# Preln attention and expert block on one core: gates multiplied into the expert activations on GpSimd, experts summed in PSUM, maxima split before they are transposed, query copy on ScalarE, statistics first

## The chip, the cores and the metric

The kernel runs on one core of a Trainium2 chip. The metric is the device time in microseconds (us) of one execution. Before the change the median of 3 executions is 1236.5 us (1234.62 to 1236.58).

## What is computed

32 batches of 256 tokens with 128 channels pass through one transformer layer: attention with 16 heads and a rational function in place of the exponential, then 4 experts of which each token takes 2.

```python
# x: 32 x 256 x 128, float32
def stablemax3(logits):                       # per head, over the keys
    x = logits - max(logits)
    s = 1 / (1 - x * (1 - 0.5 * x * (1 - x / 3)))   # x <= 0 here
    return s / sum(s)

x = x + attention(layernorm(x))               # q k^T * 8**-0.5, stablemax3, times v, w_out, b_out
xf = layernorm(x)
probs = softmax(xf @ router_w + router_b)     # 4 experts
gates = the two largest of probs, divided by their sum, zeros elsewhere
h = silu(xf @ w1[e]) * (xf @ w3[e])           # e = 0..3, 512 hidden channels each
x = x + sum_e gates[:, e] * (h[e] @ w2[e])
```

## The kernel before

Every engine has its own instruction stream, written out by hand; semaphores join them, and nothing reorders an engine's stream. The work is a pipeline over batches. Step `n` of the outer loop (`over_batches`) runs `first_half` and then `second_half` on each engine, and works on several batches at once: the queries, keys and statistics of batch n+2 or n+1, the attention of batch n, the projection, router and first expert unit of batch n-1, and the experts of batch n-2. One step is called a trip here; there are 36 of them (n = -2 to 33), and all stages are full from n = 2 to 30.

**First half of a trip.** TensorE makes, in turn, the "distances" of batch n (scores minus the row maximum, 8 units of 128x1024 into the two halves of the PSUM tile `sc`) and the expert units 1 to 7 of batch n-2 (`up_a`, `up_b`: each unit is 256 hidden channels of w1 and of w3, as three float32r products). ScalarE squares a unit of distances (`w_sq`, L464) and takes the silu of `up_a` (L472). VectorE makes the polynomial (`poly`, L603) and multiplies silu by `up_b` into `hid` (`hidden`, L595). GpSimd splits the queries and keys into a high and a low part (`qk_split`, L367 and L370); SyncE writes them to DRAM (`qk_scratch`) and reads them back in 12 transfers in the layout of `q_stack` and `k_pad`.

**Second half.** TensorE makes 8 units of scores of batch n+1 (`scores`, L963), and VectorE takes each unit's maxima (`scores_max`, L716); a later unit of scores waits for the maxima of the unit two before it. Between the scores stand the down projections of the experts of batch n-2 (`down(e)`, L982, into `up_a` or `up_b` in turn); VectorE scales each by its gate and adds it (`add_expert`, L733). VectorE aggregates the statistics (L704, L707), GpSimd and ScalarE make 1/sqrt(variance) of them and GpSimd normalizes (`xn2`, `xn`, L414). TensorE transposes `xn2` (`router_operand`, L1025). After the eighth maxima TensorE transposes `mx` (`maxima_T`, L999), VectorE splits the transposed maxima into a high and a low part (`split_maxima`, L756 and L758), and SyncE copies the two into the last rows of `q_stack`; the distances of the next first half need them. The first expert unit of batch n-1 (`up_a_unit`, `up_b_unit`) stands between `maxima_T`, `router_logits` (L1035) and `queries_operand` (L1010). ScalarE takes the logarithm of `poly` (`log_of`, L521) and its exponential (`weights_of`, L526), two units at a time, with the two small instructions of the statistics (L537, L540) between the second logarithm and the first exponential. The order of VectorE in this half is

```python
for u in range(U):
    if has(i, off + 1):
        scores_max(u)
    if u == 0:
        statistics()
    if u in (1, 3) and has(i, off - 2):
        add_expert(u // 2)
    if u == 4 and has(i, off - 1):
        router_T()
# then add_expert(2), split_maxima(), add_expert(3), route_logits(), queries_T(), the comparisons
```

## Time and profile before

| | |
|---|---|
| median of 3 executions | 1236.5 us |
| profiled execution: its own time, its span | 1235.11 us, 1233.4 us |
| TensorE busy | 1137.5 us, 92% |
| VectorE busy | 1029.9 us, 84% |
| ScalarE busy | 1015.2 us, 82% |
| GpSimd busy | 333.2 us, 27% |
| mean granted TensorE clock | 0.983 |

The profiled execution took 1235.11 us, of which 1233.4 us lie between its first and last instruction. The profile names TensorE as PE, VectorE as DVE, ScalarE as ACT, GpSimd as POOL and SyncE as SP; PEld is the weight load of TensorE, which overlaps its matmuls. The ends of matmuls are modelled in the trace: two that follow each other without a stall overlap in their rows, so a stall is best read from the distance of two starts. A float32 matmul stands as two records, with one weight load each.

### The profile page before, as it was taken

To read this page: it belongs to the slowest core of one execution; us is meant where nothing else is said; L and a number is where in the kernel's file an instruction comes from. 1 tells how busy PE (TensorE), PEld (TensorE's weight loads), DVE (VectorE), ACT (ScalarE), POOL (GpSimd) and SP (SyncE) were. 2 spreads that over 40 slices of the span, in tenths; PEclk is the share of its full clock that TensorE was granted. 3 is DMA by queue.
4 is the path that set the end of the run, shared out by engine and by line. 5 is a ranking of instruction groups with operands and counts; after the bars stand their busy time and mean duration, and the time that the engine had idled before them with its cause. 6 is when DMAs were issued, how large, how long until landed. Compare 5 with 4: busy or idle time off the path is not lost.

```text
span 1233.4 us, 29285 instructions
## 1 busy us (share of the span) xinstructions
PE 1137.5 (92%) x10116; PEld 980.6 (80%) x10116; DVE 1029.9 (84%) x1998; ACT 1015.2 (82%) x1070; POOL 333.2 (27%) x707
## 2 busy tenths in 40 slices
PE   2577999999999999999999999999999999999988
PEld 1345888888888888888888888888888888888877
DVE  3777889888888988888898888889888888988833
ACT  1478888888898888888888888898888889888872
POOL 5113322222332222233222132322312233231111
PEclk9877999999999999999999999999999999999999
DMA  5111111222111122211112221111122111121000
GB/s 173 57 56 49 44 57 57 67 65 65 46 46 48 55 65 65 65 48 43 48 55 65 65 65 51 41 48 55 65 65 65 53 40 46 56 64 62 11 6 9
DMA packets 83689, 67.97 MB, mean 55 GB/s; under 512 B 6664, under 2 KB 82120, under 8 KB 83656
## 3 DMA queue, kind: packets, MB, share of 16 engines
q1 hardware_dynamic: 83080, 67.01, 17.1%
q10 hardware_dynamic: 576, 0.52, 0.2%
q8 instruction: 20, 0.33, 0.1%
q14 instruction: 13, 0.11, 0.0%
HBM read 45.42 MB, written 20.97 MB: 54 GB/s over the span
## 4 chain that ended last, share of the span: by engine, by line
PE 59%; issue 11%; DVE 10%; POOL 7%; ACT 6%; DVEq 3%; DMA 2%; SPq 1%; POOLq 1%; ACTq 0%
PE up_a L807 13%; PE up_b L807 9%; PE sc L873 9%; PE pv L823 5%; DVE mx L716 5%; PE up_b L982 4%; PE pv L807 4%; POOL xn L414 4%; PE up_a L982 3%; DVEq L705 3%; PE sc L963 2%; DVE poly L603 2%; PE misc L1016 2%; ACT silu_a L472 2%; ACT poly L521 2%
## 5 line engine op out<-in xcount | busy, mean ns | idle before, releaser
L464 ACT ACTIVATE w_sq<-sc 128x1024 f32<-128x1024 f32 x256 | 259.2, 1026 | 142.8 <-PE sc L873 133.7
L716 DVE TENSOR_REDUCE mx<-sc 128x4 f32<-128x1024 f32 x256 | 304.6, 1214 | 41.4 <-PE sc L963 41.4
L603 DVE SCALAR_TENSOR_TENSOR poly<-w_sq,sc 128x1024 f32<-128x1024 f32 x256 | 310.7, 1215 | 33.3 <-ACT w_sq L464 26.8
L521 ACT ACTIVATE poly<-poly,two 128x2048 f32<-128x2048 f32 x128 | 251.9, 1992 | 0.4
L526 ACT ACTIVATE poly<-poly 128x2048 f32<-128x2048 f32 x128 | 239.6, 1895 | 0.0
L873 PE MATMUL sc<-q_stack,k_pad 128*128 128x256 f32 x1024 | 170.1, 294 | 7.1 <-DVE poly L603 7.0
L472 ACT ACTIVATE silu_a<-up_a 128x512 f32<-128x512 f32 x256 | 153.0, 598 | 21.2 <-PE up_a L807 14.3
L807 PE MATMUL up_a<-xn_hi,w_hi 128*128 128x256 f32 x512 | 156.1, 305 | 7.0 <-ACT silu_a L472 2.8
L873 PEld LDWEIGHTS sc<-q_stack,k_pad 128*128 128x128 f32 x1024 | 141.4, 192 | 11.8 <-DVE poly L603 9.4
L807 PE MATMUL up_a<-xn_hi,w_lo 128*128 128x256 f32 x512 | 144.4, 282 | 0.0
L807 PE MATMUL up_a<-xn_lo,w_hi 128*128 128x256 f32 x512 | 143.8, 281 | 0.0
L982 PE MATMUL up_a<-w_sb,hid 128*128 128x128 f32 x1024 | 138.7, 284 | 5.4 <-ACT silu_a L472 5.1
L381 POOL TENSOR_TENSOR x_resb<-x_res,b_out_all 128x128 f32<-128x128 f32 x64 | 27.8, 456 | 426.9 <-DVE y_acc L656 357.4
L982 PEld LDWEIGHTS up_a<-w_sb,hid 128*128 128x128 f32 x1024 | 121.3, 191 | 21.8 <-ACT silu_a L472 11.7
L963 PE MATMUL sc<-k_pad,q_stack 60*128 60x256 f32 x1024 | 105.1, 323 | 32.1 <-DMA k_pad<-qk_scratch 22.7
L823 PE MATMUL pv<-poly,v_pad 128*32 128x256 f32 x2048 | 133.1, 390 | 0.0
L982 PE MATMUL up_b<-w_sb,hid 128*128 128x128 f32 x1024 | 126.0, 277 | 0.0
L982 PEld LDWEIGHTS up_b<-w_sb,hid 128*128 128x128 f32 x1024 | 120.7, 194 | 0.0
L595 DVE TENSOR_TENSOR hid<-silu_a,up_b 128x512 f32<-128x512 f32 x160 | 108.7, 679 | 13.3 <-PE up_b L807 6.9
L963 PEld LDWEIGHTS sc<-k_pad,q_stack 60*128 60x128 f32 x1024 | 75.3, 197 | 52.2 <-DVE mx L716 14.7
L807 PEld LDWEIGHTS up_a<-xn_hi,w_hi 128*128 128x128 f32 x512 | 96.8, 189 | 18.3 <-DVE y_acc L733 10.8
L807 PEld LDWEIGHTS up_a<-xn_lo,w_hi 128*128 128x128 f32 x512 | 96.8, 189 | 0.0
(105 smaller groups left out, 2028.1 us busy)
## 6 DMA issues: line engine op xcount, KB each, us to landing
qk_scratch<-qk_split SPq DMA_DIRECT2D x32, 512.0 KB, 2.8
k_pad<-qk_scratch SPq DMA_DIRECT2D x256, 64.0 KB
q_stack<-qk_scratch SPq DMA_DIRECT2D x124, 128.0 KB
x_in<-in_L_attn_x_dram SPq DMA_DIRECT2D x32, 128.0 KB, 2.1
x_res<-in_L_attn_x_dram SPq DMA_DIRECT2D x32, 128.0 KB, 2.2
out_dram<-y_acc SPq DMA_DIRECT2D x32, 128.0 KB, 1.8
poly<-in_L_ffn_w_dram SPq DMA_DIRECT2D x2, 1024.0 KB, 6.7
q_stack<-m_split SPq DMA_DIRECT2D x64, 16.0 KB
```

The source lines that it names most:

```text
L464: nc.scalar.activation(w_sq[:, u % 2, :], sc[:, u % 2, :], ACT.Square).then_inc(sq_ok, 1)
L472: nc.scalar.activation(silu_a[:, u % 2, :], up_a[:], ACT.Silu).then_inc(silu_ok, 1)
L521: nc.scalar.activation(poly[:, C * g:C * (g + 1), :], poly[:, C * g:C * (g + 1), :], ACT.Ln, bias=two[:]).then_inc(ln_ok, 1)
L526: nc.scalar.activation(poly[:, C * g:C * (g + 1), :], poly[:, C * g:C * (g + 1), :], ACT.Exp, scale=-1.0).then_inc(p_ok, 1)
L595: nc.vector.tensor_tensor(hid[:, 2 * u:2 * u + 2, :].rearrange("p a t -> p (a t)"), silu_a[:, u % 2, :], b_bank[u], ALU.mult).then_inc(hid ...
L603: nc.vector.scalar_tensor_tensor(poly[:, u, :], w_sq[:, u % 2, :], 3.0, sc[:, u % 2, :], ALU.add, ALU.mult).then_inc(poly_ok, 1)
L716: nc.vector.tensor_reduce(by_row[:, :, 2 * g:2 * g + 2], sc[:, u % 2, :].rearrange("p (j k t) -> p j k t", j=2, k=2), AX.X, ALU.min, negat ...
L807: last = nc.tensor.matmul(dst, lhs[a], rhs[b], start=(k == 0), stop=(k == len(terms) - 1))
L823: last = nc.tensor.matmul(pv[32 * j:32 * j + 32, g // 2, :], v_pad[par][:, c, 4 * g + j, first:first + 32], poly[:, C * g + c, at:at + S], ...
L873: last = nc.tensor.matmul(sc[:, u % 2, at:at + S], k_pad[par][:, 2 * g + k, j, c * 128:(c + 1) * 128], q_stack[par][:, 2 * g + k, :], star ...
L963: last = nc.tensor.matmul(sc[:, u % 2, at:at + S], q_stack[par][rows, 2 * g + k, c * 128:(c + 1) * 128], k_pad[par][rows, 2 * g + k, j, :] ...
L982: last = nc.tensor.matmul(bank[:, c * D:(c + 1) * D], hid[:, FB * e + f, c * 128:(c + 1) * 128], w2_sb[:, FB * e + f, :], start=(f == 0), ...
```

## The change

The edits, on all five engines:

- **Gates.** The gate of a token and expert is no longer applied to the result of the down projection. VectorE makes the gates at the end of the second half of trip n (batch n-1). SyncE writes them to DRAM (`gate_scratch`) and, in the next first half, reads them back to all partitions (`gate_all`, 128 x 1024 values, 512 KB). GpSimd multiplies each of the 8 units of `hid`, 128x512, in place by the gates of its tokens; the second operand lies at a step of 8 values in `gate_all`.
- **Experts.** All four down projections add up in PSUM, chunk 0 in `up_b`, chunk 1 in `up_a`, and VectorE adds the sum once (`experts_added`) where `add_expert` had 8 instructions. `down(e)` waits for the gated units in place of `acc_ok`.
- **Maxima.** VectorE splits `mx` into `mx_split` (two instructions of 128x32) before the transposes; these then give both parts at once, one copy (`maxima_out`) takes them out of PSUM, and one transfer brings them to `q_stack` where there were two.
- **Router.** `router_logits` stands on TensorE right behind `down(3)`, ahead of `score(6)`; `route_logits` and `experts_added` stand on VectorE between the seventh and the eighth `scores_max`. `maxima_T` waits for `lg_ok` too, and `queries_operand` for `m_ok`.
- **Other moves.** The copy of queries and keys out of PSUM goes from VectorE to ScalarE, behind silu(0). `statistics()` stands ahead of the first `scores_max`. ScalarE's `exp_l` stands ahead of the last `weights_of`. GpSimd's `x_resb` goes from the first half to the end of the second.

```diff
 # SyncE, first half (at its start) and second half (at its end)
+                if has(i, off - 2):
+                    sp.wait_ge(gates_out, gates_at)
+                    after(sp, gated, gated_before)
+                    sp.dma_start(gate_all[:].rearrange("p t c e -> p (t c e)"),
+                                 row_to_all(gate_scratch, 128 * C * E)).then_inc(gates_in, 16)
...
-                    sp.wait_ge(m_hi_ok, m_split_at)
-                    sp.dma_start(q_stack[par][MROW::2, :, :].bitcast(F32),
-                                 m_split[:, 0, :].bitcast(F32)).then_inc(m_stacked[par], 16)
                     sp.wait_ge(m_ok, m_split_at)
-                    sp.dma_start(q_stack[par][MROW + 1::2, :, :].bitcast(F32),
-                                 m_split[:, 1, :].bitcast(F32)).then_inc(m_stacked[par], 16)
+                    sp.dma_start(q_stack[par][MROW:, :, :].bitcast(F32), m_split[:]).then_inc(m_stacked[par], 16)
...
+                if has(i, off - 1):
+                    par = (off - 1) % 2
+                    sp.wait_ge(gates_ok, gates_at)
+                    after(sp, gates_in, gates_read)
+                    sp.dma_start(gate_scratch, gates[par][:].rearrange("p c e -> p (c e)")).then_inc(gates_out, 16)
 # GpSimd, first half, behind the two qk_split instructions
+                if has(i, off - 2):
+                    m = no(i, off) - 2
+                    pool.wait_ge(gates_in, 16 * (m + 1))
+                    for u in range(UP):
+                        pool.wait_ge(hid_ok, UP * m + u + 1)
+                        h = hid[:, 2 * u:2 * u + 2, :].rearrange("p k (c t) -> p k c t", c=C)
+                        by_token = gate_all[:, :, :, 2 * u // FB].rearrange("p t c -> p c t")
+                        nc.gpsimd.tensor_tensor(h, h, by_token.unsqueeze(1).to_broadcast([128, 2, C, 128]),
+                                                ALU.mult).then_inc(gated, 1)
 # ScalarE, first half, behind silu(0)
+                    act.wait_ge(qk_full, m + 1)
+                    after(act, qk_ok, m)
+                    nc.scalar.copy(qk[:], misc[:]).then_inc(qk_out, 1)
 # VectorE, second half
+                def experts_added():
+                    m, par = n - 2, off % 2
+                    dve.wait_ge(down_full, m + 1)
+                    nc.vector.tensor_tensor(y_acc[par][:], up[:, :, 0:D], y_acc[par][:], ALU.add).then_inc(acc_ok, 1)
...
+                statistics()
                 for u in range(U):
                     if has(i, off + 1):
                         scores_max(u)
-                    if u == 0:
-                        statistics()
-                    if u in (1, 3) and has(i, off - 2):
-                        add_expert(u // 2)
                     if u == 4 and has(i, off - 1):
                         router_T()
-                if has(i, off - 2):
-                    add_expert(2)
+                    if u == 6 and has(i, off - 1):
+                        route_logits()
+                    if u == 6 and has(i, off - 2):
+                        experts_added()
                 if has(i, off + 1):
                     split_maxima()
-                if has(i, off - 2):
-                    add_expert(3)
-                if has(i, off - 1):
-                    route_logits()
+                if has(i, off - 1):
+                    compare()
+                if has(i, off + 1):
+                    maxima_out()
                 if has(i, off + 2):
                     queries_T()
                 if has(i, off - 1):
+                    for k in range(GATE):
+                        gate_step(k)
 # TensorE, second half
                 down(3)
+                if has(i, off - 1):
+                    router_logits()
                 score(6)
                 score(7)
...
                 if has(i, off - 1):
                     up_a_unit(i, off - 1, 0)
-                    router_logits()
                     up_b_unit(i, off - 1, 0)
```

**VectorE around the last maxima.** The instruction list of VectorE in a trip's second half, from the seventh maxima on (`mx`), in the kernel before:

```order
L716 TENSOR_REDUCE mx<-sc 128x2x2 [waits s_full] x3
L733 SCALAR_TENSOR_TENSOR y_acc<-up_a,gates,y_acc 128x128 [waits acc_ok,gates_ok,down_full]
L733 SCALAR_TENSOR_TENSOR y_acc<-up_a,gates,y_acc 128x128 [waits acc_ok]
L756 TENSOR_SCALAR m_split<-misc 16x256 [waits m_stacked1,mT_full]
L758 SCALAR_TENSOR_TENSOR m_split<-misc,m_split 16x256 [waits m_hi_ok]
L733 SCALAR_TENSOR_TENSOR y_acc<-up_b,gates,y_acc 128x128 [waits acc_ok,gates_ok,down_full]
L733 SCALAR_TENSOR_TENSOR y_acc<-up_b,gates,y_acc 128x128 [waits acc_ok]
L742 TENSOR_TENSOR logits<-misc,router_b_all 128x4 [waits gates_ok,lg_full]
L742 TENSOR_TENSOR logits<-misc,router_b_all 128x4
L746 TENSOR_REDUCE top_l<-logits 128x2 [waits lg_ok]
L749 TENSOR_TENSOR shifted<-logits,top_l 128x8 [waits exp_ok,top_ok]
```

And the same place in the changed kernel, whose first row holds the sixth and the seventh maxima:

```order
L714 TENSOR_REDUCE mx<-sc 128x2x2 [waits s_full] x2
L734 TENSOR_TENSOR logits<-misc,router_b_all 128x4 [waits gates_ok,lg_full]
L734 TENSOR_TENSOR logits<-misc,router_b_all 128x4
L738 TENSOR_REDUCE top_l<-logits 128x2 [waits lg_ok]
L741 TENSOR_TENSOR shifted<-logits,top_l 128x8 [waits exp_ok,top_ok]
L727 TENSOR_TENSOR y_acc<-up,y_acc 128x256 [waits down_full]
L714 TENSOR_REDUCE mx<-sc 128x2x2 [waits s_full]
L749 TENSOR_SCALAR mx_split<-mx 128x4x8 [waits mT_full,s_used]
L751 SCALAR_TENSOR_TENSOR mx_split<-mx,mx_split 128x4x8 [waits mx_hi_ok]
```

Five instructions (four of the router, one of the experts) now stand ahead of the eighth maxima, and two more behind it and ahead of what TensorE's transposes wait for.

**TensorE behind the last down projection.** The list of TensorE in the kernel before, from the end of `down(3)` (`w_sb`, `hid`) over the transposes of the maxima (`mx`) to the router's matmuls (`rw`):

```order
L982 MATMUL up_b<-w_sb,hid 128x128 x7
L963 MATMUL sc<-k_pad,q_stack 128x256 [waits s_used]
...
L999 MATMUL misc<-ident,mx 16x128 [waits xn2_out,s_used]
L999 MATMUL misc<-ident,mx 16x128
...
L807 MATMUL up_a<-xn_hi,w_hi 128x256 [waits xn2_lo_ok,acc_ok]
...
L1035 MATMUL misc<-rw,xn_T 128x4 [waits m_ok,xn2_out]
L1035 MATMUL misc<-rw,xn_T 128x4
```

And the same stretch in the changed kernel:

```order
L1000 MATMUL up<-w2_sb,hid 128x128 x7
L1053 MATMUL misc<-rw,xn2_T 128x4 [waits xn2_out]
L1053 MATMUL misc<-rw,xn2_T 128x4
...
L844 MATMUL pv<-poly,v_pad0 32x256 [waits p_ok]
L844 MATMUL pv<-poly,v_pad0 32x256 x7
L1018 MATMUL misc<-ident,mx_split 32x128 [waits lg_ok,mx_ok]
L1018 MATMUL misc<-ident,mx_split 32x128
L828 MATMUL up<-xn2_hi,w1_hi 128x256 [waits xn2_lo_ok,acc_ok,silu_ok]
```

The two router matmuls moved from behind the transposed maxima to ahead of the last two units of scores.

## Rows read from the trace of the kernel before

**Rows 1.** The page: span, and busy time of each engine.

```profile
span 1233.4 us, 29285 instructions
PE 1137.5 (92%) x10116; PEld 980.6 (80%) x10116; DVE 1029.9 (84%) x1998; ACT 1015.2 (82%) x1070; POOL 333.2 (27%) x707
```

**Rows 2.** Busy time in stretches: length, PE, PEld, DVE, ACT, POOL, clock.

```profile
130.50:1206.00 1075.50, 1040.39 (x9454) 905.99 (x9455) 934.35 (x1841) 933.01 (x981) 292.00 (x631) 1.00 0.17 53
```
```profile
884.00:902.00 18.00, 17.17 (x168) 13.75 (x167) 14.95 (x35) 17.55 (x14) 6.67 (x17) 1.00 0.06 16
902.00:920.00 18.00, 17.83 (x154) 16.58 (x153) 17.06 (x28) 13.95 (x20) 3.23 (x5) 1.00 0.29 95
```

**Rows 3.** Waits of the whole run: us in total, times, longest.

```profile
PEld misc L999 <- DVE mx L716: 26.0, 30, 1.8
PEld up_a L807 <- DVE y_acc L733: 10.8, 26, 0.4
```

**Rows 4.** Timeline of PE and PEld in a second half: start, length, instruction.

```profile
891.64 0.43 PE L1025 MATMUL misc<-ident,xn 128*128 128x128 f32 x2 [0.35 <-POOL xn L414]
891.91 1.95 PE L982 MATMUL up_b<-w_sb,hid 128*128 128x128 f32 x16
893.79 0.75 PE L963 MATMUL sc<-k_pad,q_stack 60*128 60x256 f32 x8
...
896.74 0.39 PE L999 MATMUL misc<-ident,mx 128*16 128x128 f32 x2 [0.35 <-DVE mx L716]
897.26 0.39 PE L807 MATMUL up_a<-xn_hi,w_hi 128*128 128x256 f32 x1
...
899.48 0.38 PE L1010 MATMUL misc<-ident,xn 128*128 128x128 f32 x2
```
```profile
898.14 0.52 PEld L1035 LDWEIGHTS misc<-rw,xn_T 128*128 128x128 f32 x4
```

**Rows 5.** Timeline of DVE, the same trip and its next first half.

```profile
892.30 0.41 DVE L692 COPY xn_T<-misc 128x256 f32<-128x256 f32 x1
...
894.33 2.36 DVE L716 TENSOR_REDUCE mx<-sc 128x4 f32<-128x1024 f32 x2 [0.49 <-PE sc L963]
...
897.17 0.41 DVE L756 TENSOR_SCALAR m_split<-misc 16x256 fp32r<-16x256 f32 x1
...
898.79 0.23 DVE L742 TENSOR_TENSOR logits<-misc,router_b_all 128x4 f32<-128x4 f32 x2 [0.25 <-PE misc L1035]
...
899.25 0.17 DVE L749 TENSOR_TENSOR shifted<-logits,top_l 128x8 f32<-128x8 f32 x1
...
919.54 0.68 DVE L595 TENSOR_TENSOR hid<-silu_a,pv 128x512 f32<-128x512 f32 x1
```

**Rows 6.** Timeline of ACT.

```profile
884.40 3.90 ACT L521 ACTIVATE poly<-poly,two 128x2048 f32<-128x2048 f32 x2
888.21 0.19 ACT L537 ACTIVATE ln_var<-var_eps 128x4 f32<-128x4 f32 x1
...
902.42 1.94 ACT L464 ACTIVATE w_sq<-sc 128x1024 f32<-128x1024 f32 x2 [0.70 <-PE sc L873]
904.25 0.60 ACT L486 COPY o_T<-pv 128x512 f32<-128x512 f32 x1
```

**Rows 7.** Timeline of POOL.

```profile
888.71 0.20 POOL L398 TENSOR_TENSOR newton<-rstd 128x4 f32<-128x4 f32 x1 [1.29 <-ACT rstd L540]
...
891.49 1.57 POOL L414 TENSOR_SCALAR xn<-x_in,mean_var,rstd 128x128 f32<-128x128 f32 x2
...
902.90 1.04 POOL L367 TENSOR_TENSOR qk_split<-qk,zero 128x512 fp32r<-128x512 f32 x1 [0.87 <-DVE qk L615]
904.02 1.30 POOL L370 TENSOR_TENSOR qk_split<-qk,qk_split 128x512 fp32r<-128x512 f32 x1
```

**Rows 8.** DMA issues: the page (KB, us to landing), SyncE's timeline.

```profile
qk_scratch<-qk_split SPq DMA_DIRECT2D x32, 512.0 KB, 2.8
```
```profile
910.79 4.93 SPq L311 DMA_DIRECT2D k_pad<-qk_scratch  x8
```

## Prediction before the run

> **What bounds the kernel now.** I read the page first for the span and the shares: TensorE is busy 92% of 1233.4 us, VectorE 84%, ScalarE 82%, GpSimd 27% [rows 1]. Shares over a run hide stages, so the busy times in stretches come next. From 130.5 to 1206.0 us the trips repeat: TensorE's wait before the transposed maxima occurs 30 times in the run [rows 3], once in each trip that has both a batch n+1 and a batch n-1 (n = 1 to 30), and 1075.5 / 30 = 35.85 us a trip, at full granted clock [rows 2]. Within one trip the two halves differ. From 902 to 920 TensorE is busy 17.83 of 18.00 us: the first half is TensorE's alone. From 884 to 902 it is busy 17.17 of 18.00 [rows 2]. So whatever a trip can lose or gain is in the second half, except for a few tenths.
>
> The timeline of TensorE shows where the second half waits. Its transposes of xn2 start at 891.64, after an idle 0.35 that GpSimd's normalization ended. The transposes of the maxima start at 896.74, after 0.35 idle for VectorE's maxima, and up_a follows only 0.52 later, where two such transposes need 0.27 (891.64 to 891.91) [rows 4]: the rest, 0.25, is the wait for add_expert(2), seen 26 times [rows 3].
>
> Who sets the 891.64? Not the statistics. ScalarE is in its two logarithms from 884.40 to 888.2 and takes ln_var right behind, at 888.21 [rows 6]; GpSimd had by then waited 1.29 us for ScalarE's result [rows 7]. From there to 891.64 it is a fixed chain of small instructions. And who sets the 896.74? From 891.64 the chain is down(3) (1.88 us, 891.91 to 893.79), scores unit 6 at 893.79, the last two maxima from 894.33, for which VectorE had sat idle 0.49 [rows 5], then the transposes. So in this half the order is: ScalarE, GpSimd, TensorE (down(3), scores), VectorE (two maxima), TensorE.
>
> **The change part by part.** I take the trip above and ask how far each of its marks moves, in us.
>
> Ahead of 891.64, nothing gained. Statistics first makes mean_var ready about 1.7 earlier, but ln_var still stands behind ScalarE's second logarithm. Down(0) no longer waits for silu(7), which lets TensorE start some 0.3 sooner; it then arrives earlier at the xn2 transposes and waits there longer. The two add_expert calls that leave VectorE's maxima 1 to 4 only lengthen its idle time before unit 6.
>
> From 891.64 to the transposed maxima, four things are put into the chain:
> - router_logits on TensorE, ahead of scores unit 6: 0.52, its four weight loads [rows 4].
> - route_logits on VectorE between maxima 6 and 7: from 898.79 to the end of the last of the four, 899.25 + 0.17 = 899.42, so 0.63 [rows 5]. Its input is ready, so no wait is added.
> - experts_added, one 128x256 sum from PSUM: 0.41, the row of the 128x256 copy out of PSUM [rows 5].
> - the split of mx, two dependent instructions of 128x32. Not in the trace. Below: two like the 128x8 row at 0.17, 0.34; above: two like the 16x256 split at 0.41, 0.82, plus a semaphore. The size is nearer the small one; I take 0.45.
>
> Together 2.0: the transposed maxima start 2.0 later, and nothing shortens that stretch, since what left VectorE had not been on it. In that time TensorE has no other work: it idles in front of them about 2.3 minus the 0.5 of the router, some 1.8.
>
> Behind it two things leave the chain before queries_operand (899.48 in the trace): the router's 0.52 between up_a and up_b, and the 0.25 of add_expert(2), since experts_added ran earlier. That is 0.77. The new wait of queries_operand for maxima_out costs nothing: the copy (0.41) lies beside up_a and up_b, 1.5 us; without that cover it would be its 0.41. So queries_operand, and with it the next first half, starts 2.0 - 0.77 = 1.2 later.
>
> The transfer of the maxima: one issue instead of two, behind a path of transposes, copy and issue that is no longer than before counted from the transposes. Since the transposes stand 0.77 nearer to the first half, the margin shrinks by this and grows by the saved issue; I count 0, with up to 0.5 on the upper side.
>
> First half. The query copy costs ScalarE 0.60, as o_T's copy of the same size, and lies in the 0.70 that ScalarE idles before its first square [rows 6], from about 902.0 on; the squares move by 0.2. VectorE loses the copy and four gate steps there, and reaches hidden(1) a tenth sooner. Since TensorE is full, I count -0.1. GpSimd gets eight products of 128x512. The gates come at about 901.5 (the query transposes at 899.48 [rows 4], a copy, four small steps); a write and a read through DRAM follow, each bounded by the 512 KB transfer at 2.8 us to landing [rows 8], so gate_all is there at about 907.5. One product: below 1.04 (second operand one repeated value), above 3.1 (the 128x128 normalization is 0.79, times four), and nearest 1.30, the row with two full operands [rows 7]; I take 1.30. Eight take 10.4, to 917.9, but the last unit of hid ends only at 920.2 [rows 5], so GpSimd ends at 921.5. Its next duty is var_eps, which ScalarE wants at 888.21 + 35.85 = 924.1. Margin 2.5 us: hidden. The limit is a product of (923.8 - 907.5) / 8 = 2.0 us.
>
> The queue of SyncE: it waits for gates_out until about 904.3, then issues gate_all, and the qk_scratch write is due at 905.3, when the split ends [rows 7]; behind it 12 stack transfers are issued until 915.7 [rows 8]. If gate_all delays these by a microsecond, they still land before the next scores at about 919.5, and behind these TensorE waits for xn2 anyway. Counted as 0; uncovered it would be at most the 2.8 of one such transfer in every trip. The edge trips are not changed by more than a few us: their down projections take 1.8 each, more than a product, so the gating keeps up.
>
> Sum: 1.2 - 0.1 = +1.1 a trip, 30 trips, +33 us. Against the profiled execution's 1235.1 that is 1268; the median of the runs shown stands 1.4 above that execution, so 1269.
>
> The Trainium skill, GPSIMD Engine Reference, section Performance pitfalls for Q7 kernels, says that a read with a step of more than 8 bytes costs about 2.9 cycles an element in place of 1.9, half as much again. No row here has a strided operand of this size. An estimate by that page: the product would take 1.3 times 1.5, about 2.0 us, right at the limit worked out above, and the sum would stay at 1269 or gain a few tenths a trip.
>
> **The rivals.**
> (B) GpSimd becomes the bound: a product takes well over 2.0 us, because of the stepped operand. For it: the 3.1 above, and the limit's closeness. Against: 1.30 in the nearest row. At 2.3 us GpSimd ends at 907.5 + 18.4 = 925.9, 2.1 past the limit, so +2.1 + 1.1 a trip: 1331. At 3.1: 932.3, +8.5 + 1.1: 1523.
> (C) Faster. The marks ahead of the transposed maxima move by less than the 0.77 that leaves the chain behind them. That is the point from which it decides. It would take router and expert instructions that cost VectorE a third of their rows' time, or an xn2 that comes earlier. The last can give at most what TensorE's idle time there gives, 0.35 + 0.3. Against it: ln_var's place behind the logarithms. If all of TensorE's waits in this half (0.3 at down(0), 0.35, 0.35, 0.25) went, it would be -1.2 a trip, 1199; half of that, 1217.
> (D) The change comes to nothing: growth ahead and gain behind balance, 1235 to 1239. For it only that small instructions in a row overlap somewhat.
>
> **How the numbers follow.** My forecast (A) has bounds of its own: lower, the split at 0.34, router and experts at two thirds of their rows, and 0.4 of waiting for xn2 gained: +0.35 a trip, 1247; upper, the split at 0.9, experts 0.6, and 0.5 for the maxima's transfer: +2.2, 1302. Chances: A 0.66, B 0.11, C 0.17, D 0.06. A measurement of this kernel can tell about 0.2% (2.5 us) from no change. Faster 0.17, same 0.06, slower 0.77. The range has to leave out no more than 0.2: from 1225, into the weaker cases of C, to 1302, which leaves out B and the strong cases of C.
>
> **What would show it.** In the profile after: the wait of the transposes on VectorE's mx_split at about 1.5 to 2 us in 30 trips; up_a right behind them without a wait for y_acc; VectorE idle about 1 us ahead of the seventh maxima; xn2's transposes still released by GpSimd, ln_var still right behind the logarithms; the product near 1.3 us and all eight done before var_eps is wanted; the first half no longer than 17.9 us. Wrong would be: a product above 2.0, ln_var waiting for GpSimd, scores waiting for k_pad, or transposed maxima less than 0.8 later against xn2's transposes than the 5.1 us now.

## Result and the profile after

The changed kernel takes 1246.7 us in the median (4 executions, 1245.46 to 1247.79) against 1236.5: the ratio is 1.0086, with a 95% interval of 1.0069 to 1.0103. It is slower, as forecast, but by 10 us and not by 33. The time lies inside the range of 1225 to 1302. The size is what missed: the measured loss is less than a third of the forecast one, and a trip lost 0.48 us where 1.1 was forecast.

The page of the changed kernel; the span and the shares, the chain that ended last, and the costliest group:

```profile
span 1245.4 us, 29490 instructions
...
PE 1112.9 (89%) x10116; PEld 975.4 (78%) x10116; DVE 960.7 (77%) x1774; ACT 1031.1 (83%) x1102; POOL 740.0 (59%) x963
...
POOL 32%; issue 20%; PE 20%; DMA 12%; DVE 9%; SPq 2%; ACT 2%; POOLq 1%; DVEq 0%
...
L396 POOL TENSOR_TENSOR hid<-hid,gate_all 128x512 f32<-128x512 f32 x256 | 410.2, 1618 | 130.2 <-DVE hid L624 75.1
```

Against [rows 1], VectorE lost 69 us of work and GpSimd gained 407. TensorE has the same 10116 matmuls and is busy less of a longer span. The chain now runs for a third through GpSimd. That looks like a verdict on the products, and it is not one, as an experiment shows below: the chain follows whatever was released last at each step, and says nothing of how close the second arrival was.

One trip, on each engine. TensorE, start and length in us; of the expert units only the first matmul of chunk 0 (904.38) and of chunk 1 (905.18) is shown:

```profile
897.46 0.44 PE L1045 MATMUL misc<-ident,xn 128*128 128x128 f32 x2 [0.82 <-POOL xn L429]
897.74 1.95 PE L1000 MATMUL up<-w_sb,hid 128*128 128x128 f32 x16
899.52 0.51 PE L1053 MATMUL misc<-rw,xn_T 128*128 128x4 f32 x4
899.96 0.74 PE L984 MATMUL sc<-k_pad,q_stack 60*128 60x256 f32 x8
900.63 1.93 PE L844 MATMUL pv<-poly,v_pad 128*32 128x256 f32 x32
904.23 0.40 PE L1018 MATMUL misc<-ident,mx_split 128*32 128x128 f32 x2 [1.67 <-DVE mx_split L751]
904.38 0.36 PE L828 MATMUL up<-xn_hi,w_hi 128*128 128x256 f32 x1
...
905.18 0.28 PE L828 MATMUL up<-xn_hi,w_hi 128*128 128x256 f32 x1
...
905.90 0.38 PE L1030 MATMUL misc<-ident,xn 128*128 128x128 f32 x2
...
908.00 1.29 PE L894 MATMUL sc<-q_stack,k_pad 128*128 128x256 f32 x8
...
933.71 0.43 PE L1045 MATMUL misc<-ident,xn 128*128 128x128 f32 x2 [0.84 <-POOL xn L429]
```

VectorE in the same second half:

```profile
900.51 1.22 DVE L714 TENSOR_REDUCE mx<-sc 128x4 f32<-128x1024 f32 x1 [1.01 <-PE sc L984]
901.65 0.22 DVE L734 TENSOR_TENSOR logits<-misc,router_b_all 128x4 f32<-128x4 f32 x2
...
902.18 0.42 DVE L727 TENSOR_TENSOR y_acc<-up,y_acc 128x256 f32<-128x256 f32 x1
902.52 1.21 DVE L714 TENSOR_REDUCE mx<-sc 128x4 f32<-128x1024 f32 x1
903.76 0.18 DVE L749 TENSOR_SCALAR mx_split<-mx 128x32 fp32r<-128x32 f32 x1
```

ScalarE and GpSimd at the end of the next first half:

```profile
926.48 3.90 ACT L550 ACTIVATE poly<-poly,two 128x2048 f32<-128x2048 f32 x2
930.28 0.19 ACT L566 ACTIVATE ln_var<-var_eps 128x4 f32<-128x4 f32 x1
```
```profile
926.61 1.54 POOL L396 TENSOR_TENSOR hid<-hid,gate_all 128x512 f32<-128x512 f32 x1 [0.68 <-DVE hid L624]
928.10 0.21 POOL L407 TENSOR_TENSOR var_eps<-mean_var,eps_all 128x4 f32<-128x4 f32 x1
```

Compared stretch by stretch with [rows 4] and [rows 5], and with the start of the first distances before, at 901.57 in this row:

```profile
901.57 0.70 PE L873 MATMUL sc<-q_stack,k_pad 128*128 128x256 f32 x3
```

| from, to | before | after | difference | mean of 26 trips: before | after | difference |
|---|---|---|---|---|---|---|
| xn2 transposes, scores unit 6 | 2.15 | 2.50 | +0.35 | 2.15 | 2.49 | +0.34 |
| scores unit 6, transposed maxima | 2.95 | 4.27 | +1.32 | 2.96 | 4.27 | +1.31 |
| transposed maxima, queries_operand | 2.74 | 1.67 | -1.07 | 2.78 | 1.66 | -1.12 |
| queries_operand, first distances | 2.09 | 2.10 | 0 | 2.09 | 2.23 | +0.14 |
| xn2 transposes, first distances | 9.93 | 10.54 | +0.61 | 9.98 | 10.65 | +0.67 |
| first distances, next xn2 transposes | | 25.71 | | 25.87 | 25.67 | -0.20 |

The means are taken from the starts of the same instructions in the 26 trips between the third and the 29th of the 32 xn2 transposes, called the steady part here. The length of a trip is read from the first and the last start of these transposes (54 records, two a trip); before and after:

```profile
L1025 PE MATMUL misc<-ident,xn x54: 272/298/328, 174.5 to 1106.9; 128*128 128x128 f32 x54
```
```profile
L1045 PE MATMUL misc<-ident,xn x54: 272/298/330, 170.8 to 1115.6; 128*128 128x128 f32 x54
```

(1106.9 - 174.5) / 26 = 35.86 us and (1115.6 - 170.8) / 26 = 36.34 us: +0.48 a trip, 12.4 us in all. Ahead of the steady part the changed kernel is 3.7 us shorter, behind it 3.3 us longer (129.8 against 126.5), and the span grew by 12.0. The same measure is used for all kernels below, with what lies behind the steady part, the tail, beside it. The part ahead of it, 170 to 177 us in these traces, runs in places at a lower granted clock (0.75 from 40 to 100 us before, 0.73 after); there is one trace of each kernel, so its differences of a few us are not explained here.

In the tail the products are not hidden. In the last two trips there are no distances, the gates arrive late, and the eight products follow each other without a pause; ScalarE then waits for GpSimd, for 1.86 us where it waited for 0.53 before:

```profile
1201.04 12.42 POOL L396 TENSOR_TENSOR hid<-hid,gate_all 128x512 f32<-128x512 f32 x8 [5.04 <-DMA gate_all<-gate_scratch]
```
```profile
1213.64 0.20 ACT L566 ACTIVATE ln_var<-var_eps 128x2 f32<-128x2 f32 x1 [1.86 <-POOL var_eps L407]
```

### The profile page after: what moved, and what is told of

Same layout as the page of the kernel before. It is cut to its first block, busy times and chain, and to the rows that moved or that the text cites. A ratio compares the mean times of both kernels' runs of the same rounds, so it can differ in the third digit from the quotient of the medians.

```text
span 1245.4 us, 29490 instructions
## 1 busy us (share of the span) xinstructions
PE 1112.9 (89%) x10116; PEld 975.4 (78%) x10116; DVE 960.7 (77%) x1774; ACT 1031.1 (83%) x1102; POOL 740.0 (59%) x963
## 4 chain that ended last, share of the span: by engine, by line
POOL 32%; issue 20%; PE 20%; DMA 12%; DVE 9%; SPq 2%; ACT 2%; POOLq 1%; DVEq 0%
POOL hid L396 25%; DMA gate_all<-gate_scratch 9%; PE up L828 6%; PE up L1000 5%; DVE mx L714 5%; POOL xn L429 4%; DMA gate_scratch<-gates 2%; PE sc L984 1%; PE sc L894 1%; ACT poly L550 1%; PE misc L1045 1%; PE pv L844 1%; PE misc L1018 1%; SPq L324 1%; PE misc L1053 1%
## 5 line engine op out<-in xcount | busy, mean ns | idle before, releaser
L396 POOL TENSOR_TENSOR hid<-hid,gate_all 128x512 f32<-128x512 f32 x256 | 410.2, 1618 | 130.2 <-DVE hid L624 75.1
L1000 PE MATMUL up<-w_sb,hid 128*128 128x128 f32 x2048 | 256.2, 279 | 0.6 <-POOL hid L396 0.6
L828 PE MATMUL up<-xn_hi,w_hi 128*128 128x256 f32 x832 | 245.9, 296 | 1.6 <-DVE y_acc L727 1.1
L1000 PEld LDWEIGHTS up<-w_sb,hid 128*128 128x128 f32 x2048 | 240.0, 193 | 8.5 <-POOL hid L396 0.8
L828 PE MATMUL up<-xn_hi,w_lo 128*128 128x256 f32 x832 | 234.4, 282 | 0.0
L828 PE MATMUL up<-xn_lo,w_hi 128*128 128x256 f32 x832 | 233.7, 281 | 0.0
L496 ACT ACTIVATE silu_a<-up 128x512 f32<-128x512 f32 x256 | 153.0, 598 | 20.1 <-PE up L828 11.8
L828 PEld LDWEIGHTS up<-xn_hi,w_hi 128*128 128x128 f32 x832 | 157.1, 189 | 5.4 <-issue 2.4
L828 PEld LDWEIGHTS up<-xn_lo,w_hi 128*128 128x128 f32 x832 | 157.3, 189 | 0.0
L828 PEld LDWEIGHTS up<-xn_hi,w_lo 128*128 128x128 f32 x832 | 156.1, 188 | 0.0
```

What stands on the lines that cost most here:

```text
L396: nc.gpsimd.tensor_tensor(h, h, by_token.unsqueeze(1).to_broadcast([128, 2, C, 128]), ALU.mult).then_inc(gated, 1)
L496: nc.scalar.activation(silu_a[:, u % 2, :], up_a[:], ACT.Silu).then_inc(silu_ok, 1)
L828: last = nc.tensor.matmul(dst, lhs[a], rhs[b], start=(k == 0), stop=(k == len(terms) - 1))
L1000: last = nc.tensor.matmul((up_b, up_a)[c][:, 0:D], hid[:, FB * e + f, c * 128:(c + 1) * 128], w2_sb[:, FB * e + f, :], start=(e == 0 and f ...
```

## Experiments

Two theories stood against each other. T: what the change puts ahead of the transposed maxima in the second half costs the time, and the products on GpSimd are hidden. G: the products and the gate transfers set the time. Each kernel was timed against the kernel before, on the same chip.

**No products.**

```diff
-                    for u in range(UP):
-                        pool.wait_ge(hid_ok, UP * m + u + 1)
-                        h = hid[:, 2 * u:2 * u + 2, :].rearrange("p k (c t) -> p k c t", c=C)
-                        by_token = gate_all[:, :, :, 2 * u // FB].rearrange("p t c -> p c t")
-                        nc.gpsimd.tensor_tensor(h, h, by_token.unsqueeze(1).to_broadcast([128, 2, C, 128]),
-                                                ALU.mult).then_inc(gated, 1)
...
-                    pe.wait_ge(gated, UP * m + FB // 2 * (e + 1))
+                    pe.wait_ge(hid_ok, UP * m + FB // 2 * (e + 1))
```

> The changed kernel without the eight products on GpSimd (the gates are not applied to the experts at all); the down projections wait for hid alone, and the two gate transfers still run. Theory T: GpSimd's next duty was reached 2.0 us before ScalarE's answer was there, so nothing changes: 1245 to 1248 us, up to 2 less from the first and last trips. Theory G: the time falls by more than 10 us, to the kernel before's or under it.

Measured: 1247.5 us, ratio 1.0093 (1.0073 to 1.0113), the changed kernel's time. The products, a quarter of the chain by the page's line for them, were taken away and nothing came of it: a steady trip takes (1116.7 - 170.1) / 26 = 36.41 us against 36.34 in the changed kernel, and only the tail is 2.3 us shorter. As far as it names the products, G falls. The gate transfers still run in this kernel; they run in router_back below too, which takes the old kernel's time with them.

**Contiguous gates.**

```diff
-                        by_token = gate_all[:, :, :, 2 * u // FB].rearrange("p t c -> p c t")
+                        e = 2 * u // FB
+                        by_token = gate_all[:].rearrange("p t c e -> p (t c e)")[:, e * S:(e + 1) * S].rearrange(
+                            "p (c t) -> p c t", c=C)
```

> The changed kernel whose products read their second operand from consecutive addresses of gate_all (the numbers are then another token's gates). If the step of 32 bytes makes a product slower, it falls from 1.62 to about 1.30 us, the time of the split with two full operands; if not, it stays at 1.62. The time of the kernel stays at 1245 to 1249 either way, since the products are hidden.

Measured: 1245.8 us, ratio 1.0081 (1.0065 to 1.0096). The groups of this kernel show the product at 1.29 us:

```profile
L398 POOL TENSOR_TENSOR hid<-hid,gate_all 128x512 f32<-128x512 f32 x256 | 328.4, 1290 | 200.9 <-DVE hid L626 146.2 <-DMA gate_all<-gate_scratch 54.5
```

So the step of 32 bytes costs 0.33 us on 512 elements, a quarter more. Without it the product is the 1.30 of [rows 7]. The time does not care: a steady trip is the same (36.34), the tail 2.1 us shorter.

**Slow products.**

```diff
+                        nc.gpsimd.tensor_tensor(idle_out[:, u, :], zero[:].to_broadcast([128, S]),
+                                                zero[:].to_broadcast([128, S]), ALU.add)
                         nc.gpsimd.tensor_tensor(h, h, by_token.unsqueeze(1).to_broadcast([128, 2, C, 128]),
```

> The changed kernel with one more GpSimd instruction of about 0.61 us (a 128x256 sum of zeros) ahead of each of the eight products, so 2.3 us a unit in place of 1.62. The prediction's limit for a product was 2.0 us. By the changed kernel's rows the first unit starts at 912.8, so eight end at about 931.2, where ScalarE wants GpSimd's first statistics result by 930.2: 1.0 to 1.5 us more a trip, 1275 to 1295 us. If GpSimd's products were hidden with any margin, no change, 1245 to 1250.

Measured: 1266.1 us, ratio 1.025 (1.0216 to 1.0283). The expectation of 1275 to 1295 was too high. The added instruction took 0.628 us, a unit 2.24 us. A steady trip takes (1123.1 - 173.4) / 26 = 36.53 us, 0.19 more than in the changed kernel, or 5 us of the 18 by which the span grew; between 205 and 1100 us ScalarE waits for var_eps in 10 of 25 trips, 3.0 us together. So the limit is only just reached at 2.24 us a unit. Most of the rest, 10.3 us, is in the tail (140.1 us against 129.8), where the products were not hidden before either; 2.6 us lie ahead of the steady part.

**Router back.** The router's matmuls, logits and comparisons stand behind the transposed maxima again, and experts_added behind the split.

```diff
                     if u == 4 and has(i, off - 1):
                         router_T()
-                    if u == 6 and has(i, off - 1):
-                        route_logits()
-                    if u == 6 and has(i, off - 2):
-                        experts_added()
                 if has(i, off + 1):
                     split_maxima()
+                if has(i, off - 2):
+                    experts_added()
+                if has(i, off + 1):
+                    maxima_out()
                 if has(i, off - 1):
+                    route_logits()
                     compare()
-                if has(i, off + 1):
-                    maxima_out()
 # TensorE: router_logits() between up_a_unit and up_b_unit again; ScalarE: exp_l behind the last weights_of
```

> The changed kernel with the router's matmuls, logits and comparisons back behind the transposed maxima, and experts_added behind the split of the maxima; everything else as changed. Theory T (what stands ahead of the transposed maxima in the second half costs the time; the products on GpSimd are hidden): from the changed kernel's traces 0.35 us (router on TensorE) and 0.87 us (logits, experts) leave the stretch ahead of the transposes, and some 0.6 + 0.2 come back behind them, so 0.3 to 0.5 us less in each of 30 trips: 1232 to 1238 us against 1246.7. Theory G (the products and the gate transfers, through which a third of the changed kernel's chain runs, set the time): no change, 1245 to 1248.

Measured: 1235.8 us, ratio 0.9994 (0.9984 to 1.0004), as theory T had it: the kernel before's time, 11 us less than the changed kernel. A steady trip: (1103.5 - 173.4) / 26 = 35.77, 0.57 less than in the changed kernel (0.3 to 0.5 were expected) and 0.09 less than in the kernel before. The tail is 134.0 us, 7.5 more than in the kernel before, in a profiled execution that was the slowest of ten (1239.6 us). By this pair the loss comes from the router, its comparisons and experts_added, which were moved together; experts_later below moves the last alone.

**Router and split back.** As above, and the maxima are transposed unsplit, as in the kernel before, with experts_added ahead of the split.

```diff
-                        last = nc.tensor.transpose(misc[0:2 * H, c * 128:(c + 1) * 128],
-                                                   mx_split[:, c].rearrange("p j h g -> p (j h g)").bitcast(F32), ident[:])
+                        last = nc.tensor.transpose(misc[0:H, c * 128:(c + 1) * 128], mx[:, c, :], ident[:])
 # VectorE: m_split from misc in two steps; SyncE: two transfers, as before the change
```

> As router_back, and the maxima too are transposed unsplit and split behind the transposes, with two transfers, as before the change. Theory T: another 0.44 us leaves the stretch ahead of the transposes; experts_added stands ahead of the split, so up_a waits about 0.2 us for it. 0.3 to 0.5 us a trip less than router_back: 1220 to 1228 us, faster than the kernel before. If the two transfers arrive too late for the first distances, the gain is lost there: 1232 to 1238. Theory G: 1245 to 1248.

Measured: 1233.4 us, ratio 0.9972 (0.9962 to 0.9982), against the 1220 to 1228 of theory T: this expectation missed. A steady trip takes (1100.1 - 171.9) / 26 = 35.70, only 0.07 less than in router_back. The time fits the expectation's other case, 1232 to 1238, but not its reason: the first distances start 2.09 us behind the query transposes in each trip, as in the kernel before, so the transfers are not late. TensorE's rows say why. With the split maxima (router_back) and with the unsplit ones (this kernel):

```profile
894.40 0.39 PE L1017 MATMUL misc<-ident,mx_split 128*32 128x128 f32 x2 [0.80 <-DVE mx_split L751]
895.58 0.51 PE L1054 MATMUL misc<-rw,xn_T 128*128 128x4 f32 x4
896.74 0.38 PE L1029 MATMUL misc<-ident,xn 128*128 128x128 f32 x2
```
```profile
890.80 0.39 PE L1012 MATMUL misc<-ident,mx 128*16 128x128 f32 x2 [0.36 <-DVE mx L718]
892.23 0.58 PE L1048 MATMUL misc<-rw,xn_T 128*128 128x4 f32 x4
893.47 0.38 PE L1023 MATMUL misc<-ident,xn 128*128 128x128 f32 x2
```

From the transposed maxima to the router is 1.18 us in the one and 1.43 in the other; to the query transposes 2.34 and 2.67. The router's matmuls write where the transposed maxima lie, so they wait until VectorE has taken these out: one copy in the first case, two dependent steps in the second. Of what the split costs ahead of the transposes (0.44) it gives 0.33 back behind them in these two trips, 0.38 in the mean of 26. Against the kernel before, a steady trip of router_split_back is 0.16 shorter and the tail 5.3 us longer.

**Experts later.** The changed kernel, experts_added behind the split.

```diff
-                    if u == 6 and has(i, off - 2):
-                        experts_added()
                 if has(i, off + 1):
                     split_maxima()
+                if has(i, off - 2):
+                    experts_added()
```

> The changed kernel with one move: experts_added stands behind the split of the maxima, in place of between the seventh and eighth maxima. Theory T: 0.35 us leaves the stretch ahead of the transposes, and up_a, which now starts 0.15 after them, waits for it about 0.2 us longer: net 0.1 to 0.2 us a trip less, 1241 to 1244 us. Theory G: no change, 1246 to 1248.

Measured: 1245.8 us, ratio 1.0081 (1.0059 to 1.0103). That is above the 1241 to 1244 that T expected, and the interval holds the changed kernel's 1.0086, so the time does not tell T from G. The steady trip speaks for T: (1111.6 - 170.2) / 26 = 36.21, 0.13 less, inside T's 0.1 to 0.2. In the three kernels above that keep the changed kernel's order it is 36.34, 36.34 and 36.41, so the step is twice what these differ by, and rests on one trace. The stretches say where it comes from: scores unit 6 to the transposes 3.96 (4.27 in the changed kernel), to queries_operand 1.89 (1.66), to the first distances 2.10 (2.23).

**Old router ahead.** The kernel before with one part of the change.

```diff
                 down(3)
+                if has(i, off - 1):
+                    router_logits()
                 score(6)
 # VectorE: route_logits() between maxima 6 and 7; maxima_T waits for lg_ok, queries_operand for m_ok
```

> The kernel before with one part of the change: router_logits behind down(3), and route_logits between the seventh and eighth maxima. Theory T (stretches count one by one between the xn2 transposes and the next first half): 0.34 (TensorE) and 0.52 (the four VectorE steps, without experts_added) go in ahead of the transposed maxima, and 0.76 leaves between up_a and queries_operand, 0.52 of work and some 0.2 in which the router waited for the split maxima. Net +0.1 us a trip, +3 us: 1237 to 1242. By the prediction's own sum (0.52 + 0.63 ahead, 0.52 behind) it is +0.6 a trip, 1253 to 1257.

Measured: 1280.3 us, ratio 1.0357 (1.0333 to 1.038). Both expectations were far too low. Two things were not foreseen. First, a wait that the router's matmuls had covered: up_b now waits for add_expert(3), behind the two steps of the split. Second, TensorE's clock. Steady trips alternate between 36.83 and 38.26 us, as in the starts of three successive xn2 transposes:

```profile
889.81 0.43 PE L1025 MATMUL misc<-ident,xn 128*128 128x128 f32 x2 [0.51 <-POOL xn L414]
...
928.07 0.43 PE L1025 MATMUL misc<-ident,xn 128*128 128x128 f32 x2 [0.36 <-POOL xn L414]
...
964.91 0.43 PE L1025 MATMUL misc<-ident,xn 128*128 128x128 f32 x2 [0.50 <-POOL xn L414]
```

The shorter trips show the first thing alone: they are 0.97 over the kernel before, and from the transposed maxima to queries_operand they take 2.74 us, as in the kernel before (2.74 and 2.83 in turn), though the router has left this place. The other 1.43 in every second trip is the clock. The transposes, up_a and up_b in a trip where it falls, and up_b in the next, where it does not:

```profile
895.82 0.39 PE L999 MATMUL misc<-ident,mx 128*16 128x128 f32 x2 [0.91 <-DVE mx L716]
896.33 0.39 PE L807 MATMUL up_a<-xn_hi,w_hi 128*128 128x256 f32 x1
...
897.86 0.36 PE L807 MATMUL up_b<-xn_hi,w_hi 128*128 128x256 f32 x1 [0.55 <-DVE y_acc L733]
...
936.02 0.36 PE L807 MATMUL up_b<-xn_hi,w_hi 128*128 128x256 f32 x1 [0.45 <-DVE y_acc L733]
```

and the stretches around it (length; PE, PEld, DVE, ACT, POOL busy; granted clock; DMA):

```profile
896.00:898.00 2.00, 1.32 (x9) 0.94 (x8) 1.61 (x6) 1.98 (x3) 0.00 (x0) 1.00 0.00 0
898.00:900.00 2.00, 2.00 (x16) 1.44 (x20) 0.43 (x3) 1.64 (x2) 0.00 (x0) 0.58 0.28 82
900.00:901.50 1.50, 1.50 (x17) 0.46 (x10) 0.33 (x4) 0.00 (x0) 0.87 (x4) 0.50 0.31 87
901.50:904.00 2.50, 2.50 (x24) 2.09 (x28) 1.32 (x3) 0.85 (x1) 0.67 (x2) 0.95 0.00 0
```

The granted clock falls from 1.00 to 0.50 (2.4 to 1.2 GHz) for some 3 us. It does so in every second trip; the same stretch in four trips that follow each other:

```profile
822.90:826.50 3.60, 3.60 (x25) 2.00 (x26) 0.76 (x5) 1.64 (x2) 0.96 (x5) 0.55 0.28 82
860.40:864.00 3.60, 3.15 (x30) 2.26 (x29) 1.14 (x7) 2.52 (x4) 0.86 (x4) 1.00 0.26 78
897.90:901.50 3.60, 3.60 (x25) 2.00 (x26) 0.76 (x5) 1.74 (x2) 0.87 (x4) 0.56 0.28 82
935.40:939.00 3.60, 3.15 (x31) 2.18 (x29) 1.24 (x7) 2.62 (x4) 0.76 (x4) 1.00 0.23 69
```

In the two trips with the fall (mean granted clock 0.55 and 0.56) TensorE has 25 matmuls in 3.6 us of work, at full clock 30 or 31 in 3.15.

**Old router ahead, second.** add_expert(3) ahead of the split.

```diff
                 if has(i, off - 2):
                     add_expert(2)
+                    add_expert(3)
                 if has(i, off + 1):
                     split_maxima()
-                if has(i, off - 2):
-                    add_expert(3)
```

> old_router_ahead with add_expert(3) ahead of the split of the maxima instead of behind it, so that up_b finds its bank free. In old_router_ahead up_b waited 0.5 us for it in each trip, which ate what the router's matmuls gave back when they left that place, and TensorE's clock fell to half for some 3 us in every second trip. If that wait is the first part of the miss, a trip without a clock fall takes 36.2 to 36.4 us in place of 36.8. If the clock falls only behind two idle times in a row (in front of the transposes and again in front of up_b), it no longer falls: 1246 to 1254 us. If the longer idle time alone does it, it still falls in every second trip: 1265 to 1272.

Measured: 1241.7 us, ratio 1.0048 (1.0031 to 1.0064): 39 us less for where one call stands. A steady trip: (1111.8 - 173.1) / 26 = 36.10, at a granted clock of 1.00. Both numbers lie below what was expected (1246 to 1254, and 36.2 to 36.4). Of the 1.45 us between this trip and the mean one of old_router_ahead, 37.55, half is the wait (36.83 - 36.10 = 0.73) and half the clock (37.55 - 36.83 = 0.72). So the router ahead costs the old kernel 0.24 us a trip, once the wait and the clock fall that it set off are gone.

**Query copy and statistics.** Two parts of the change undone in router_split_back, one at a time.

```diff
 # query_copy_vector: ScalarE's copy behind silu(0) is taken out
+                if has(i, off + 1):
+                    m = n + 1
+                    dve.wait_ge(qk_full, m + 1)
+                    after(dve, qk_ok, m)
+                    nc.vector.tensor_copy(qk[:], misc[:]).then_inc(qk_out, 1)
 # stats_second
-                statistics()
                 for u in range(U):
                     if has(i, off + 1):
                         scores_max(u)
+                    if u == 0:
+                        statistics()
```

> router_split_back with the query copy back on VectorE, in the first half. The prediction counts the copy's move at about nothing, at most a tenth of a us a trip: 1231 to 1237 us against 1233.4. If ScalarE's copy costs time there, this is faster, under 1230.

Measured: 1237.6 us, ratio 1.0011 (1.0002 to 1.0021), against 0.9972: 4 us slower, just outside of what was expected of a move that costs nothing, and not faster. A steady trip is the same to 0.03 us, (1103.5 - 174.5) / 26 = 35.73 against 35.70. Of the 4.0 us between the two spans, 2.6 lie ahead of the steady part (174.5 against 171.9); why is open.

> router_split_back with the statistics behind the first maxima, as before the change. By the prediction their place gains nothing while ScalarE takes them behind two logarithms: 1232 to 1236 us against 1233.4. If they set the xn2 transposes, 0.5 us a trip and more is lost: over 1247.

Measured: 1235.3 us, ratio 0.9991 (0.9977 to 1.0005), as expected. A steady trip: (1103.5 - 174.9) / 26 = 35.72, the same to 0.02; here too the part ahead of the steady trips is longer, by 3.0 us.

**ScalarE's order.** The prediction says that the xn2 transposes wait for ln_var, which waits behind two logarithms. This edit was tried on the kernel before, and on router_split_back:

```diff
                     log_of(0)
-                    log_of(1)
...
                     nc.scalar.activation(rstd0[:, s], ln_var[:, s], ACT.Exp, scale=-0.5).then_inc(rstd0_ok, 1)
+                if has(i, off):
+                    log_of(1)
```

> The kernel before with the two small statistics instructions of ScalarE between its two logarithms instead of behind both. If ScalarE's order sets the xn2 transposes, as the prediction says, they come up to 1.0 us sooner, less what TensorE is then still busy (it idles 0.35 to 0.5 there): 0.4 to 0.6 us a trip, 1218 to 1226 us. If the statistics of VectorE set them, nothing: 1234 to 1239.

Measured: 1225.5 us, ratio 0.9919 (0.9906 to 0.9933). A steady trip: (1094.8 - 173.3) / 26 = 35.44 us, 0.42 less than before, as expected. In this kernel ScalarE waits 0.76 us for GpSimd's var_eps, so here the place of the statistics would count:

```profile
877.99 0.21 ACT L536 ACTIVATE ln_var<-var_eps 128x4 f32<-128x4 f32 x1 [0.76 <-POOL var_eps L392]
```

> router_split_back with ScalarE's two small statistics instructions between its logarithms. Here the statistics stand first on VectorE, so variance and epsilon are ready when the first logarithm ends; the xn2 transposes wait 0.8 us on TensorE and that wait should go: 0.7 to 1.1 us a trip less than router_split_back's 1233: 1200 to 1213. If the products on GpSimd, which end at about the same time, take their place as what is waited for, less: 1215 to 1228.

Measured: 1212.7 us, ratio 0.9814 (0.9798 to 0.9831), the upper end of the expectation and the fastest kernel of this study. A steady trip: (1081.4 - 170.2) / 26 = 35.05, 0.65 less than in router_split_back, just under the expected 0.7 to 1.1. The statistics stand first here, and ln_var no longer waits for var_eps. Its stretch from 205 to 1100 us has TensorE busy 885.85 of 895.00 us:

```profile
205.00:1100.00 895.00, 885.85 (x8088) 772.15 (x8088) 757.78 (x1379) 807.46 (x869) 573.62 (x739) 1.00 0.23 72
```

That leaves 9 us, 1%, in which TensorE has no row.

## Why the prediction was right in sign and wrong in size

**What bounds the kernel.** Right. The xn2 transposes are still released by GpSimd and those of the maxima by VectorE. That ScalarE's order sets the first is shown: moving ln_var alone gained 11 us on the old kernel, and the place of the statistics gained nothing in a steady trip while ln_var stood where it was.

**The sum, term by term**, in the mean of the steady trips:

| | forecast | measured |
|---|---|---|
| four terms ahead of the transposed maxima | +2.0 | +1.65 |
| what leaves behind them | -0.77 | -1.12 |
| transfer of the maxima | 0 | +0.14 |
| first half | -0.1 | -0.20 |
| a trip (by its whole length) | +1.1 | +0.48 |

The step that failed is the net of the second half, 2.0 - 0.77 = 1.2, measured 0.53: both of its terms were off by 0.35, and both the same way. The rest of the miss is the count: 30 full trips were charged, while the 26 steady ones gave 12.4 us, and the parts ahead and behind came to -0.4 together.

**The four terms ahead of the transposed maxima.** In the trip shown 1.67. The router on TensorE: 0.52 predicted, 0.35 measured. Logits, experts and split: 0.63 + 0.41 + 0.45 = 1.49 predicted, 0.53 + 0.34 + 0.45 = 1.32 measured. So the split was right. The others were mis-sized alike: I took durations where an in-order engine costs only the distance of two starts. The next instruction begins before the row of the last has ended. experts_added has a row of 0.42 us, and the next starts 0.34 after it.

**"Behind it two things leave the chain ... That is 0.77."** In the trip shown 1.07. Three matmuls of the kernel before, the last of up_a, the router's and the first of up_b:

```profile
897.95 0.28 PE L807 MATMUL up_a<-xn_hi,w_lo 128*128 128x256 f32 x1
898.17 0.58 PE L1035 MATMUL misc<-rw,xn_T 128*128 128x4 f32 x4
898.69 0.36 PE L807 MATMUL up_b<-xn_hi,w_hi 128*128 128x256 f32 x1
```

From the transposes to up_a it is 0.15 us and no longer 0.52: 0.37 gone where 0.25 was counted, since the second transpose overlaps what follows. From the last matmul of up_a to the first of up_b it was 0.74 and is 0.12 (905.06 to 905.18): 0.62 gone where 0.52 was counted. The last 0.07 lie within up_b, whose first two matmuls stand 0.12 apart and not 0.20. Part of the 0.62 is a wait of the router: it starts 0.22 behind up_a's last matmul, where such matmuls follow each other by 0.12, because it waits for the split of the maxima; the list of instructions in the section on the change shows `m_ok` among what it waits for. In the kernel before and in router_split_back, which splits in two steps, the router starts 1.43 us behind the transposes, although up_a starts at 0.52 in the one and at 0.38 in the other. So the split sets the router's start there, and taking add_expert(2) away alone would have gained nothing at this place: its 0.25 is a gain only because the router left too.

**The transfer of the maxima**, counted at 0 with up to 0.5 above: in the trip shown it is 0, in the next the first distances start 0.2 later behind the query transposes than before (942.14 to 944.44), 3.0 us after SyncE's issue at 941.44. Over 26 trips the distance is 2.09 in each trip of the kernel before, of router_back and of router_split_back, and 2.09 to 2.38 here. The margin is used up, as the prediction feared, at a mean price of 0.14. No run took away the transfer alone. For it speak experts_later, where the query transposes stand 0.23 later behind those of the maxima and the distance is 2.10 again, and a trip at the end of the changed kernel, where the profile itself names the transfer:

```profile
942.14 0.38 PE L1030 MATMUL misc<-ident,xn 128*128 128x128 f32 x2
...
944.44 1.19 PE L894 MATMUL sc<-q_stack,k_pad 128*128 128x256 f32 x8
...
1162.36 1.19 PE L894 MATMUL sc<-q_stack,k_pad 128*128 128x256 f32 x8 [1.05 <-DMA q_stack<-m_split]
```
```profile
941.44 0.70 SPq L342 DMA_DIRECT2D q_stack<-m_split  x1
```

**First half**, -0.1 predicted, -0.20 measured: the right sign, and half of what it was.

**GpSimd's products.** The price was too low, 1.30 against 1.62, and in the steady trips it did not matter: the last product ended at 928.15, var_eps was ready at 928.3, and ScalarE asked for it at 930.28. The margin was 2.0 us, 2.5 predicted. The limit of 2.0 us a unit was nearly right: at 2.24 ScalarE waited in 10 of 25 trips, and a trip grew by 0.19. "The gating keeps up" in the last trips was wrong: the eight products stand there back to back, and without them the tail is 2.3 us shorter. The rule of the Trainium skill, GPSIMD Engine Reference, section Performance pitfalls for Q7 kernels, has the sign and not the size here: it gives half as much again for a read with a step above 8 bytes, and this product, with one of its two operands so stepped, costs 25% more. The prediction's estimate by it, 2.0 us, would have stood at the limit.

**Range and rivals.** B did not happen, and G, its stronger form, is refuted for the steady trips. C's condition, less than 0.77 ahead, was far from met, though what was gained behind was more than it reckoned with. The measured 1246.7 lies at the lower bound of forecast A, 1247. That is in part luck: the terms named for this bound (0.34 for the split, two thirds of 0.52, 0.63 and 0.41, less 0.77, 0.1 and 0.4) add up to +0.1 and not to the +0.35 a trip that the prediction has.

## What to carry to other kernels

A chain through an in-order engine is priced by distances between starts, and a step that is moved is priced by what its old place waited for too, not only by its own work. A step put into a queue may cover a wait for the step behind it: take it away and that wait appears. Where a net is the difference of two larger sums, an error of 0.35 us in each doubled it here, so the range should be made from the sums and not from the net. A time per trip is taken from full trips only: an average that holds the shorter last ones hides what the end costs. The engine on which the chain of waits spends most of its time is not thereby the one to speed up: ask how late the second arrival was, and look at small instructions that stand behind large ones on an engine which nobody called the bound.

## What the runs showed of the hardware

TensorE's granted clock fell to half in old_router_ahead, in every second trip, for about 3 us, behind two idle stretches in the falling trip that is shown (0.91 us before the transposes and 0.55 before up_b in TensorE's rows). The next trip has the same two, of 0.91 and 0.45 us, and did not fall. Nor did it fall in the steady trips of the changed kernel, which idle 0.82 us before the xn2 transposes and 1.67 before those of the maxima, nor in old_router_ahead_2, where the second stretch is gone (granted clock 1.00 from 173 to 1112 us). Why it fell in one trip of two is open. It cost 1.43 us each time, about half of the 39 us between the two kernels.

A GpSimd product of 128x512 takes 1.29 us with both operands contiguous and 1.62 with one at a step of 32 bytes.

VectorE starts its next instruction before the row of the last has ended: 0.34 us from start to start for a row of 0.42 (128x256 from PSUM), 0.53 from the router's first small instruction to what follows its fourth, where the prediction took 0.63 from the first start to the last end.
